# A four-layer graph network on one core: operands made in an earlier layer, column ends in two parts, h read back by pairs, weight maxima through TensorE

## The reference

```python
h = max(layernorm(x), 0); x = x + relu((Dinv (adj + I) Dinv) @ h @ W0)          # layer 0
h = max(layernorm(x), 0); x = x + (D1 adj D1) @ h @ W1.T + b1                   # layer 1
h = max(layernorm(x), 0); x = x + relu((Dinv (adj + I) Dinv) @ h @ W2)          # layer 2
h = max(layernorm(x), 0)                                                        # layer 3
e = where(adj != 0, exp(-leaky_relu(s_left + s_right)), 0)
x = x + sigmoid(attn_a * (e / sum(e) @ h @ W_sa) + attn_b * (adj @ h @ W_g + b_g))
```

## Time and profile before

| | |
|---|---|
| time, three runs | 1852.32 us median (1850.20 to 1856.18) |
| the profiled execution | 1852.62 us, of which the traced span is 1850.8 us |
| TensorE busy | 1721.5 us, 93% of the span |
| VectorE, ScalarE, GpSimd busy | 1110.7, 776.0, 615.2 us |
| granted TensorE clock, mean | 0.971 of full |
| DMA | 402.71 MB, mean 218 GB/s |

### The profile page before, as it was taken

The page is one execution under the profiler, slowest core; times in us unless marked ns, Lnnn a source line. Parts: engine busy times, 40 slices in busy tenths (PEclk is TensorE's granted clock), DMA queues, the critical chain, the costliest instruction groups (busy, mean ns, idle before and its releaser), DMA issues.

```text
span 1850.8 us, 31682 instructions
## 1 busy us (share of the span) xinstructions
PE 1721.5 (93%) x12852; PEld 1174.5 (63%) x12852; DVE 1110.7 (60%) x1953; ACT 776.0 (42%) x1187; POOL 615.2 (33%) x572
## 2 busy tenths in 40 slices
PE   3999989799799898799999999999999899999996
PEld 1444436457577776668888897878787644444454
DVE  5776656568887787434333443553641566877765
ACT  5674443444444444313222231210100466767655
POOL 0001130257667765502223130111200345545431
PEclk9999999899899999889999999999999999999998
DMA  9984736597679866986575698766553443444423
GB/s 394 360 291 137 230 93 206 177 348 250 243 272 327 288 236 221 346 307 210 164 258 174 224 323 311 258 236 227 196 161 127 147 124 91 148 128 120 146 82 125
DMA packets 166999, 402.71 MB, mean 218 GB/s; under 512 B 18212, under 2 KB 57504, under 8 KB 163120
## 3 DMA queue, kind: packets, MB, share of 16 engines
q1 hardware_dynamic: 166852, 400.68, 63.5%
HBM read 289.44 MB, written 111.17 MB: 216 GB/s over the span
## 4 chain that ended last, share of the span: by engine, by line
PE 64%; DVE 9%; DMA 4%; ACT 3%; POOL 3%; issue 2%; SPq 1%; ACTq 0%; POOLq 0%; DVEq 0%
PE ps L1036 13%; PE ps L1069 11%; PE ps L1070 11%; PE ps L1071 11%; PE ps L1116 6%; PE ps L1117 6%; PE ps L1118 6%; DVE U L1362 3%; DMA Ad<-U 2%; DMA U<-in_adjT 1%; ACT U L1678 1%; DVE CT L1401 1%; DVE stage L1345 1%; DMA HB<-in_w 0%; POOL Q L1878 0%
## 5 line engine op out<-in xcount | busy, mean ns | idle before, releaser
L1069 PE MATMUL ps<-U,HB 128*128 128x256 f16 (+2 forms) x2520 | 640.7, 262 | 29.0 <-DVE CT L1401 12.1
L1070 PE MATMUL ps<-U,HB 128*128 128x256 f16 (+2 forms) x2520 | 640.6, 262 | 0.0
L1071 PE MATMUL ps<-U,HB 128*128 128x256 f16 (+2 forms) x2520 | 640.3, 262 | 0.0
L1116 PE MATMUL ps<-U,HB 128*128 128x512 f16 (+3 forms) x960 | 343.7, 361 | 33.5 <-DVE U L1362 21.7
L1362 DVE SCALAR_TENSOR_TENSOR U<-U,cS 128x512 f16<-128x512 f32 (+7 forms) x273 | 269.7, 1009 | 167.2 <-ACT U L1678 166.4
L1118 PE MATMUL ps<-U,HB 128*128 128x512 f16 (+3 forms) x960 | 343.5, 360 | 0.0
L1117 PE MATMUL ps<-U,HB 128*128 128x512 f16 (+3 forms) x960 | 343.4, 360 | 0.0
L1036 PE MATMUL ps<-W,OT 128*128 128x512 f16 (+1 forms) x1320 | 302.5, 383 | 11.1 <-DVE xr L1428 7.6
L1678 ACT ACTIVATE U<-U,cS 128x512 f16<-128x512 f32 (+7 forms) x273 | 214.5, 811 | 198.2 <-PE ps L1118 51.8
L1069 PEld LDWEIGHTS ps<-U,HB 128*128 128x128 f16 x2520 | 248.4, 99 | 62.0 <-issue 14.7
L1070 PEld LDWEIGHTS ps<-U,HB 128*128 128x128 f16 x2520 | 248.6, 99 | 27.5
(11 more groups left out here) (203 smaller groups left out, 1925.0 us busy)
## 6 DMA issues: line engine op xcount, KB each, us to landing
U<-in_adjT SPq DMA_DIRECT2D x289, 256.0 KB, 3.6
U<-Ad SPq DMA_DIRECT2D x72, 896.0 KB, 5.9
Ad<-U SPq DMA_DIRECT2D x40, 896.0 KB, 5.6
HB<-HBd SPq DMA_DIRECT2D x44, 512.0 KB, 6.8
xd<-xr SPq DMA_DIRECT2D x84, 256.0 KB, 4.6
xr<-xd SPq DMA_DIRECT2D x84, 256.0 KB, 5.5
U<-in_adj SPq DMA_DIRECT2D x14, 1354.0 KB, 8.4
HBd<-stage SPq DMA_DIRECT2D x16, 896.0 KB, 6.5
```

Source lines behind the costliest of these rows:

```text
L1069: eng.matmul(o, h[0], hi, start=J == 0 and a == 0, stop=False)
L1070: eng.matmul(o, h[0], lo, start=False, stop=False)
L1071: last = eng.matmul(o, h[1], hi, start=False, stop=to in "acg" and J == 9 and a == 1)
L1116: eng.matmul(o, h[0], hi, start=j == 0, stop=False)
```

## The change

- `AHEAD` names 20 pairs of layer 1: j = 0, 2, 4, 6 of group 6, j = 0, 2, 4 of groups 7 to 10, j = 0, 2, 4, 10 of group 11. They are no longer made on the fly. From step (2, 1) on, one pair every 8.5 us of TensorE's own time is fetched, summed (5.2 us after its fetch), split (8 and 9 us) and stored (12.5 us), while layer 0 runs, in places of its own (`pre`); layer 1 then reads them back as layers 2 and 3 do.
- The maxima of the weights of layers 1 to 3 and of the gate weights are spread over a 128 x 128 tile by DVE, multiplied with the identity on TensorE (`w_top`, `gate_top`) and reduced by DVE from PSUM. GpSimd keeps only the one of layer 0's weight.
- `evacuate` of groups 6 to 23 ends after the five DVE instructions and the ACT copies; the four subtractions are a stage of their own, `settle`, 2 us later. Until `evacuate` has been put, no split of the next group beyond its first pair is put.
- `restore` takes one pair J for all seven slots (one DMA of 896 KB), each as its tiles are done with; pairs 6 and 7 only at steps 4 and 8 of the next layer's first group.
- Adding the diagonal on GpSimd (`eye`) is a stage of its own, up to 7 steps ahead of its step, instead of being part of the split.
- The projections are placed anew (`at_us`): the narrow group takes three, its last one moves into the group behind it; gates are placed earlier; some loads of x are earlier. The h of pair 10 is split by fewer, longer instructions (`ends`). Pairs of h are at least 16 us (layer 1) or 12 us apart instead of 8. Scores, masks and splits of the attention pass go by time as well as by steps. The places in `U` follow from all this.

```diff
+AHEAD = [(g, j) for g in range(GW, 12) for j in
+         ((0, 2, 4, 6) if g == GW else (0, 2, 4) if g < 11 else (0, 2, 4, 10))]
...
+    for n, (g, j) in enumerate(AHEAD):
+        u = later(AT["agg", 2, 1], 8.5 * n)
+        for us, *stage in ((0, "fetch", "pre", g, j), (0, "fetch", "pre", g, j + 1), (5.2, "sums", g, j), (8, "split", g, j),
+                           (9, "split", g, j + 1), (12.5, "a_keep", g, j)):
+            plan(later(u, us), *stage)
...
     def near(key, u, steps, us):
-        return AT[key] <= (later(u, us) if winograd(key[1]) else u + steps)
+
+        g, j = SEQ[u][1:] if 0 <= u < len(SEQ) else (0, 0)
+        if winograd(g) and winograd(key[1]) and key[1] > g and steps <= LA:
+            return key[2] < 2 and ("evacuate", g) not in s.no or ("evacuate", g) in s.no and AT[key] <= later(u, us)
+        return AT[key] <= (later(u, us) if winograd(key[1]) else max(u + steps, later(u, us)) if key[1] >= GE else u + steps)
...
-        while split < len(splits) and near(splits[split], u, LA, 9.6):
+        while eyed < len(eyes) and near(eyes[eyed], u, LA if eyes[eyed][1] < 2 else LA + 3, 13):
+            if not have(("fetch",) + eyes[eyed]):
+                break
+            put("eye", *eyes[eyed][1:])
+            eyed += 1
+        while split < len(splits) and near(splits[split], u, LA, 10.4 if splits[split][1] >= GE else 9.6):
...
-        quiet = later(u, 8)
-        if J == 7:
-            for slot in range(7):
-                plan(max(later(u, 14), AT["agg", 6 * l - 1, 17]), "restore", l, slot, 1)
+        quiet = later(u, 8 if J >= 7 else 16 if l == 1 else 12)
+        if J < 8:
+            late = AT["agg", 6 * l, 4 * J - 20] if J > 5 else AT["agg", 6 * l - 1, max(2 * J + 2, 11 + J if l == 1 else 0)]
+            plan(max(later(u, 24), late), "restore", l, J)
...
+        at_us = {0: (9, 13, 17, 21), 4: (9, 14, 19), 5: (3, 10, 15)}.get(c, (12, 18.5, 25, 31.5))
...
             put("evacuate", g)
+            if winograd(g):
+                plan(later(u + 1, 2), "settle", g)
...
+                    opened(TOPBANK)
+                    eng.matmul(ps[TOPBANK][:, 0:P], colb[:, 0, :], identf[:, 0, :], start=True,
+                               stop=True).then_inc(s_wall if of else s_gall, 1)
+                    free[TOPBANK] = [after]
...
-                    pool.wait_ge(s_wmax, s("w_max", n))
-                    eng.partition_all_reduce(wm[:, 1, n:n + 1], wm[:, 0, n:n + 1], P, RMAX).then_inc(s_wall, 1)
...
-                elif kind == "split":
+                elif kind == "eye":
...
+                    eng.dma_start(HB[:, :, J, :, :].rearrange("p s h n -> p s (h n)"),
+                                  HBd[l][0:7, :, J, :, :].rearrange("s p h n -> p s (h n)")).then_inc(s_hb[J], 16)
```

More of the change, by code:

```diff
@@ L236, in schedule @@
     scores = [k for k in splits if k[1] >= GE]
+    eyes = [k for k in splits if on_diagonal(*k[1:]) and (k[1] < GW or 12 <= k[1] < GE and k[2] >= 20)]
     def plan(u, *stage):
@@ L251, in ahead @@
     def ahead(u):
-        nonlocal fetched, split, summed, scored, masked
-        while scored < len(scores) and AT[scores[scored]] <= u + 6 and scored < masked + 2:
+        nonlocal fetched, eyed, split, summed, scored, masked
+        while scored < len(scores) and near(scores[scored], u, 6, 15.6) and scored < masked + 2:
             if not have(("row_out", scores[scored][1]), *free_of("sc_a")):
@@ L257, in ahead @@
             scored += 1
-        while masked < scored and AT[scores[masked]] <= u + 5 and masked < s.count.get("split_e", 0) + 3:
+        while masked < scored and near(scores[masked], u, 5, 13) and masked < s.count.get("split_e", 0) + 3:
             if not have(("fetch",) + scores[masked], *free_of("em"), *free_of("acc")):
@@ L303, in fetch_to, with weights @@
             fetched += 1
-    def weights(u, n):
-        late = 4 if n else 2
-        for d, kind in ((0, "w_fetch"), (3, "w_max"), (4 + late, "w_hi"), (5 + late, "w_lo"), (9 + late, "w_keep")):
-            if kind != "w_keep" or n:
-                plan(u + d, kind, n)
+    def weights(n, g, *js):
+        kinds = ("w_fetch", "w_max", "w_top", "w_hi", "w_lo", "w_keep") if n else ("w_fetch", "w_max", "w_hi", "w_lo")
+        for kind, j in zip(kinds, js):
+            plan(AT["agg", g, 0] + j if g else AT["agg", 0, 15] + j, kind, n)
     def pair(u, l, J):
@@ L739, in gnn_kernel @@
         filled_u, filled_ft, filled_st = [0] * (NU + 1), [0, 0], [0, 0]
-        for _, g, j in in_order("fetch"):
-            if j == NT - 1 and not fly(g, j):
+        for what, g, j in in_order("fetch"):
+            if what == "pre":
+                q = LANE["rt", g, whole(j)]
+                filled_u[q] += 16
+                LOADED["pre", g, j] = s_u[q], filled_u[q]
+            elif j == NT - 1 and not fly(g, j):
                 filled_st[g % 2] += 16
@@ L1671, in _ @@
                     if j < NT - 1:
-                        for at_free in slot_free(free_of("un", g, whole(j)) if winograd(g) else free_of("sp", g, j)):
+                        place = "sp" if not winograd(g) else "pre" if made_ahead(g, j) else "un"
+                        for at_free in slot_free(free_of(place, g, whole(j) if winograd(g) else j)):
                             act.wait_ge(*at_free)
```

258 lines of the change are left out of this document (158 added, 100 removed).

## The result

| | before | after |
|---|---|---|
| median of four runs | 1853.7 us (1850.2 to 1856.2) | 1823.76 us (1822.68 to 1826.1) |
| ratio, 95% interval | | 0.9842 [0.9821, 0.9862] |
| traced span | 1850.8 us | 1824.3 us |
| TensorE busy | 1721.5 us | 1710.0 us |
| granted clock, mean | 0.971 | 0.983 |

A forecast was written before the change was run, and what follows sets the result against it. TensorE, busy 93% of the span, was taken as the bound, its waits nearly all ended by DVE. 1852.6 - 21 - 45 - 16 - 3 + 2 = 1769.6, about 1770 us; 8-in-10 range 1744 to 1806 us.

The forecast's parts named there:

- Layer 0: Groups 2 to 5: of 30 us lost in groups 3 to 5, 9 stay lost (bounds 3 and 30), gain 21 us.
- all three stalled stretches: Layer 0: product maxima and diagonals as own stages together remove the causes of every stalled stretch there.
- all fit, DVE being at about 87%: Layer 0: the 20 pairs' added work fits on DVE (load 58%), ACT (42%) and GpSimd (29%).
- 9 us of the 30 as lost: Layer 0: part of the old loss kept because DMA queues would be nearly full (0.97); bounds 3 and 30.
- a sign of being wrong: Profile after: layer 0 split waits ended by ACT behind GpSimd behind a fetch, layer 1 waits, or TensorE waiting for the spread.
- (a): End of layer 0: DMA becomes the bound, layer 0 keeps 30 us of losses, 1795 us; chance 0.13.
- (b): Layer 1: losses come from the chain, not load; keeps 36 of 61 us, 1790 to 1800 us; chance 0.10.
- (c): Layer 0, ACT's queue: late fetches stop TensorE; slower if all 20 pairs cost over 4.3 us each; chance 0.04.
- (d): Whole kernel: each stall is replaced by the next late thing, no change, 1845 to 1855 us; chance 0.03.
- Layer 1 and group 12: Fewer pairs on the fly, `near`, `settle` and spread restores: 16 of 61 us stay lost (bounds 6 and 36), gain 45.
- Layer 3: Groups 19 to 24: earlier gates and group 24's splits; 6 of 22 us stay lost (bounds 2 and 14), gain 16.
- The product maxima: Layer 0: five products of about 0.4 us each added on TensorE, +2 us; GpSimd's standing after all-reduces gone.

The follow-up runs named there:

- no_ahead: Changed kernel with the list of pairs made ahead left empty, all 60 pairs of layer 1 made on the fly: 1824.7 us.
- product_only: Kernel before with only the five maxima made by products with the identity, at the steps where the change puts them: 1843.8 us.
- thin_both: Changed kernel with VectorE's low halves and GpSimd's sums of the 20 pairs made in 16 columns only, output not the reference's: 1796.3 us.
- thin_lo: Changed kernel with VectorE's low halves of the 20 pairs made in 16 columns only, output not the reference's: 1806.2 us.
- twelve: Changed kernel with 12 pairs made ahead instead of 20, pairs 0 and 2 of groups 6 to 11, one each 13 us: 1834.6 us.
- thin_sums: Changed kernel with GpSimd's sums of the 20 pairs made in 16 columns only, output not the reference's: 1807.0 us.
- fetch_first: Changed kernel with sums, splits and store of each pair made ahead 3 us later behind its fetches: 1821.8 us.
- max_on_pool: Changed kernel with the five maxima of weights and gate left on GpSimd as partition_all_reduce: 1855.9 us.

## Why the prediction was wrong, step by step

The sum was 21 + 45 + 16 + 3 - 2. By stretches it was:

- **Layer 0, forecast 21 us of gain, measured 16 of loss (and 2 more in groups 0 and 1, within what these differ by between kernels).** This is the step that failed. Its parts on maxima and diagonals were right in kind: without the pairs layer 0 takes 233.0 us (no_ahead), 15 gained, 10 of them with the maxima alone (product_only); but they remove half of the 30 us, not "all three stalled stretches". The failed sentence is "all fit, DVE being at about 87%", the term "9 us of the 30 as lost". The 20 pairs cost 31 us, all of it by VectorE's low halves and GpSimd's sums (thin_both). The sentence added busy shares and asked only whether they pass 1. First, the shares were too low: the 58% are of the 182.5 us that were to shrink; of the 227 us forecast for groups 2 to 5, VectorE's 149.5 us and the pairs' 56 are some 90%. And the two engines' shares were taken as separate, while the sums stretch VectorE's splits from 837 to 1019 ns. Second, the test was the wrong one: operands are due within 10.4 us, and ScalarE and VectorE take turns in them in order. With VectorE busy 66% of groups 2 to 5 (154.6 of 232.7 us, thin_both) nothing more is late than without the pairs; with 70% (thin_lo) 10 us more are lost, with 73% (twelve) 21, with 77% (thin_sums) 13, with 79% (after) 31. Time is lost far below 1, and the share alone does not order the cases. That it is the lead of 10.4 us which is too short is argued: no run made it longer. The upper bound, 30 us lost, was exceeded: 46 of clean time. A bound "all that was lost before" is none for work that is added. Nor did a sign of being wrong name what came: TensorE's waits for splits in layer 0 are ended by VectorE (30.0 us at L1454), not by ScalarE behind GpSimd behind a fetch.
- **The rivals.** (a) had the right stage and the wrong resource, and its 1795 is still 29 us short; with a DMA share of 0.86 nothing was lost, and the forecast share of 0.97 was 0.76. (b) came near in size: layer 1 with group 12 kept 30.5 of its 61 us, where (b) gave 36 and the forecast 16; but not by its route, since only 1.6 us of TensorE's waits in groups 6 to 11 of after are for an operand, the others for banks, pair 10 and h. (c) had the right route, ScalarE's queue, but wanted late fetches (fetch_first: no); its "7 with the clock's half rate" does not follow from 85 us over 20 pairs, since a slower clock makes a wait dearer, so that fewer microseconds of it are enough. (d) is ruled out by the time. The result is a mixture that none of them priced: a loss per pair of 1.6 us and not 4.3, from VectorE and GpSimd. The prediction did name GpSimd's sums, but not that they could slow VectorE; in the earlier trace rows a 128x1024 split takes 1525 ns, in the timeline above 1.2 us alone.
- **Layer 1 and group 12, forecast 45, measured 30.5.** The part on the load was right: the pairs gone bring 31 us, more than any other part. The waits named fell too: `CT` to 0.6 us, pair 10 to 4.5 us (0 to 6 given), ScalarE's waits for the write-backs from 42.1 us in 15 to 26.4 in 6. The size was off: 25.5 us stay in groups 6 to 11 (345.9 against 320.4) and 5 in group 12, in place of 16. 20.0 of the 25.5 are idle (345.9 - 325.86), most of it in five waits for the projections' banks (9.0 us), one more of them (2.8) and pair 10 (4.5); the rest is the clock behind them. And it was put down to the wrong parts: the rule in `near`, `settle` and the restores, which were to end these waits, together with the rest of the change take 5 us in groups 6 to 11 (no_ahead: 377.3 against 371.9) and give 4 in group 12.
- **Layer 3, forecast 16, measured 13.7.** Right: no wait for the gates' bank, groups 19 to 22 from 63.1, 64.7, 62.6, 42.1 to 60.9, 61.3, 61.3, 33.8 us. Some 3 us of group 22's 8 only moved, with a projection, into the group behind it (the clean groups 16 and 17: 36.9 and 44.5 to 33.8 and 47.2). Group 24, which was to start earlier, kept its 75 us.
- **The last groups, forecast 3, measured 0** (320.5 us from group 25 to the end of the span in both).
- **The product maxima** were priced at their place, not by themselves; the runs give 10 us alone and 32 with the pairs.
- **The range.** Its lower end does not follow from its bounds: 1769.6 - 6 - 10 - 4 - 1 = 1748.6, not 1744. Its upper bounds together (30, 36 and 14 us kept, no gain in the last groups, 3 us for `gate_top`) come to 1824.6, close to the time measured, but by luck: layer 0 lost 46 and not 30, the others less than their bounds.

By the traced spans 26.5 us came of the 83. Of the 56 missing, layer 0 has 37, layer 1 with group 12 has 14.

## What to carry to other kernels

Work moved into "free" time of an in-order engine is not free because the busy shares sum below 1: here 20 pairs cost 31 us with VectorE busy 79% of the stretch, and 12 pairs 21 us at 73%. Ask how late they make what is due soon. And VectorE's and GpSimd's times were not separate where VectorE's instruction read two tensors of SBUF and GpSimd read too: price them together. When a part moves work from one stage to another, measure both stages: the total alone (1824.7 against 1823.8 us) would have said that the 20 pairs do nothing, while they move 31 us each way.

## What the runs showed of the hardware that was not expected

- A VectorE split with two SBUF inputs took 837 ns on average in layer 0 without the pairs' work, 1019 with the pairs' GpSimd subtractions, 868 with GpSimd fills of the same total length; a GpSimd subtraction of 128x256 went from 0.72 to 1.59 us beside a split.
- `partition_all_reduce` took 0.4 us, and GpSimd stood 64 us in groups 2 to 5 of max_on_pool, around five of them, at nothing that the profile shows: 7.1 to 12.9 us behind each, and 6.2 to 6.8 before each of three.
- DMA at a share of 0.86 of 16 engines over 233 us (297 GB/s) disturbed neither VectorE (808 ns a split) nor TensorE.
